# Graph and expert layer on one Trainium2 core: the slots of the routing's deviations and of the early rows' search

## Chip, core and metric

The kernel runs on one core of one Trainium2 chip. The metric is the device time of one execution in microseconds (us), the median of several runs.

## The reference

x is 4096 x 128, adj is 4096 x 4096 with few nonzero entries, thinly spread but denser in the first rows; all in fp32.

```python
h = layernorm(x)
filt = tanh(adj * adj) * (adj > 0)
vals, idx = top_k(filt, 350)                      # only rows with more than 350 entries lose any
new_adj = zeros.at[rows, idx].set(vals where kept)
x = x + relu(new_adj @ (tanh(h @ W_proj + b_proj) @ W_gcn) + b_gcn)
h = layernorm(x)
scores = h @ Wg.T + bg                            # 8 experts, best 2, softmax over the two
x = x + sum over e of combine[e] * (relu(h @ W1[e].T + b1[e]) @ W2[e].T + b2[e])
```

## The kernel before

**First stage: the adjacency in 64 chunks.** Rows of the output are worked in 8 blocks of 512 (`NB`), and each block needs 8 chunks (`NK`) of 512 x 512 of the adjacency. Chunk n, 1 MB, is loaded by SP into one of four buffers (`abuf`) once ACT has squared and DVE has marked chunk n - 4. ACT squares it (L1088) and takes the tanh (L1092) into `tbuf`, also four buffers; PE multiplies it by the features `g_sb`, four accumulating fp32 products of 128 x 512 (L1349); DVE marks its positive entries (`mark_positive`, L855 for a block's first chunk, L858 for the others), for the count of entries of each row. Every engine's program is written out by hand as a loop over **slots**, `for n in range(FFN)`, where slot n has chunk n and what else is due in that slot. Engines meet at semaphores alone, and each works strictly in the order of its own program. ACT squares chunk n + 1 in its slot n.

**Early rows.** Rows with over 350 entries need the exact top 350. They lie in the first block. Four of them are fetched, and a search of 15 steps (`STEPS`) finds each one's threshold, two bits a step: on DVE `raise_threshold` (L719, L721) takes the result of the step before, and `count_candidates` (L708, L712, L715) counts for three candidates; PE adds the counts up over the row's partitions (`total_candidates`, L1279), in the middle of the chunk's products in the same slot. Steps run in slots `STEP0` = 18 to 32. In slot `TIE` = 33 DVE counts the ties; in TIE + 1 it masks the rows (`mask_rows`, L735 to L740); in TIE + 2 PE turns them at the slot's head (`turn_rows`, L1289); in TIE + 3 and TIE + 4 it multiplies them by `g_sb` ahead of the chunk (`row_features`, L1294, 32 matmuls a slot); ACT copies the result in TIE + 4 (`features_out`, L1126), PE turns it in TIE + 6, and DVE writes it over the four columns of the features in TIE + 7 (`write_features`, L751). The first block itself is routed fifth and waits for this.

**Routing a block.** Once a block's features are finished, it is routed beside the chunks of later blocks. `ORDER` has the blocks, `START` the slot in which each begins: 19, 27, 35, 43, 47, 51, 58, 65. Blocks are counted here from 0, so routed block 2 is the third. From its START on, by slots: +0 PE turns the features (`features_back`, L1240); +1 DVE adds them to x, takes the statistics (L771, L775) and works out the deviations in 15 small linked instructions (`norm_scale`, L381 to L394); +2 DVE normalises the rows (`normalise`, L786), ahead of that slot's marks, and cuts them into two fp16 halves behind them (`cut_rows`, L798, L800); +3 PE turns them at the slot's head, and ACT copies them (L1138, L1140); +4 PE takes the gate's scores at the head (`gate`, L1320), DVE the best expert (`choose`, L805 to L812); +5 DVE the second, ahead of the marks (`choose_second`), ACT the exponential (L1144); +6 PE counts the places (`places`, L1327 to L1334), DVE the probabilities and the rows' slots in memory (`probabilities`, `assign`, L823 to L836). Then POOL scatters the block's rows with eight indirect DMAs (L623) to where the experts' tiles are read.

**Second stage: the experts.** After six blocks `first_tiles` on DVE, in slot `FIRST` = 58, works out the first 17 tiles of 256 rows. SP loads them into the place of `abuf` (L433, L435), after the marks of chunk 60. 39 tiles follow on PE (L1436 to L1458), from 319.4 us on, with the last two blocks' routing beside them. The results are scattered, loaded and added.

In a slot DVE has this order: `ready_steps` (a step of the search, `normalise`, `choose_second`), then `mark_positive`, then the rest (`route_steps`, and `first_tiles` last). PE has `row_features` and `route_steps` ahead of the chunk.

Of the kernel before, what the change touches and what calls it, by code (L numbers as in the profile page):

```python
# [7 lines left out]
CK = 4  # L8
# [6 lines left out]
def gnn_moe_layer(nc, x, adj_tiles, adj_rows, w_proj, b_proj, w_gcn, b_gcn,  # L15
# [43 lines left out]
    ORDER = list(range(1, NB // 2 + 1)) + [0] + list(range(NB // 2 + 1, NB))  # L59
    START = [19, 27, 35, 43, 47, 51, 58, 65]  # L60

    AT_ADD, AT_NORM, AT_TURN, AT_COPY, AT_GATE = 1, 2, 3, 3, 4
    AT_CHOOSE, AT_SECOND, AT_EXP, AT_PLACE, AT_PROB, AT_ASSIGN = 4, 5, 5, 6, 6, 6
    OUT = 1
    FIX = NK + OUT + 2
    STEP0 = FIX + 7
    TIE = STEP0 + STEPS
    FFN = NCH + 1

    COUNT = 2  # L70
    END = START[-1] + AT_ASSIGN + 1
    FIRST = START[SIX - 1] + AT_ASSIGN + 1
    NOWHERE = 1 << 20

    xs = nc.dram_tensor("routed_rows", (E * RS + TS, ROW), fp32).ap()
# [3 lines left out]
    with ctx:  # L79
# [576 lines left out]
        def _(dve):  # L656
            chain = [s_dve, 0]

            def link(ins):

                chain[1] += 1
                ins.then_inc(chain[0], 1)
                dve.wait_ge(chain[0], chain[1])
# [102 lines left out]
            def add_features(i, b, rs):  # L766
                at = space(i)

                dve.wait_ge(rs.r1, i + 1)
                xb = xres[:, b * SUB:(b + 1) * SUB, :]  # L770
                dve.tensor_tensor(xb, xb, at.x2[:, :].rearrange("p (c d) -> p c d", c=SUB), ALU.add  # L771
                                  ).then_inc(rs.x2, 1)
                dve.wait_ge(rs.x2, i + 1)
                for cc in range(SUB):
                    last = dve.bn_stats(stats[:, b * SUB + cc, :], xres[:, b * SUB + cc, :])  # L775
                link(last)
                norm_scale(dve, link, b * SUB, SUB).then_inc(rs.ns, 1)

            def normalise(i, b, rs):
# [163 lines left out]

            def ready_steps(n):

                if STEP0 < n <= TIE:
                    raise_threshold(early, 0, n - STEP0 - 1)
                if STEP0 <= n < TIE:
                    count_candidates(early, 0, n - STEP0)
                if n == TIE:  # L950
                    count_ties(early, 0)
                for i, b in enumerate(ORDER):
                    if n == START[i] + AT_NORM:
                        normalise(i, b, routed)
                    if n == START[i] + AT_SECOND:
                        choose_second(i, b, routed)

            def route_steps(n):
                for i, b in enumerate(ORDER):
                    if n == START[i] + AT_ADD:  # L960
                        add_features(i, b, routed)
                    if n == START[i] + AT_NORM:
                        cut_rows(i, routed)
                    if n == START[i] + AT_CHOOSE:
                        choose(i, b, routed)
                    if n == START[i] + AT_PROB:
                        probabilities(i, routed)
                    if n == START[i] + AT_ASSIGN:
                        assign(i, routed)

            for n in range(FFN):
# [54 lines left out]
            with dve.If(redo > 0):  # L1026
                chain[:], before_if = [s_dve2, 0], chain[:]
                dve.wait_ge(s_yo, NT)
                for i in range(2):
                    dve.wait_ge(routed.scat[i], NB // 2 * Q * 16)  # L1030
                link(dve.tensor_copy(base[:, :], base_i[:, :]))
                dve.tensor_tensor(key[:, :], flags[:, :], rowidf[:, :], ALU.mult).then_inc(s_key, 1)
                dve.wait_ge(s_keyrow, 16)
                link(dve.tensor_scalar(keyflag, keyrow, 0.0, None, ALU.is_gt))
                link(dve.tensor_reduce(nflag[:, :], keyflag, AX.X, ALU.add))

                link(dve.tensor_scalar(nflag[:, :], nflag[:, :], 1.0 / R, 0.5 - 0.5 / R, ALU.mult, ALU.add))
                dve.tensor_scalar(nrounds[:, :], nflag[:, :], 1.0, None, ALU.max).then_inc(s_nr, 1)
                rounds = read_rounds(dve)
                with dve.Fori(0, rounds) as r:  # L1040
                    pick_rows(general, r, keyrow)
                    square_rows(general, r)
                    for b in range(STEPS):
                        count_candidates(general, r, b)
                        raise_threshold(general, r, b)
                    count_ties(general, r)
                    mask_rows(general, r)
                    rows_turned(general, r)
                    write_features(general, r)
                dve.memset(tmp[:, :], 0.0).then_inc(s_fixed, 1)  # L1050
                dve.wait_ge(s_fixed, 1)
                dve.wait_ge(s_xre, 16)
                for i, b in enumerate(ORDER):
                    add_features(i, b, rerouted)
                    normalise(i, b, rerouted)
                    cut_rows(i, rerouted)
                    choose(i, b, rerouted)
                    choose_second(i, b, rerouted)
                    probabilities(i, rerouted)
                    assign(i, rerouted)  # L1060
                    if i == SIX - 1:
                        first_tiles()
                last_tiles()
                for t in range(NT, 2 * NT):
                    cut_h(t, t % 2)
                chain[:] = before_if
# [9 lines left out]
        def _(act):  # L1076
# [74 lines left out]

            def route_steps(n):
                for i in range(NB):
                    if n == START[i] + AT_COPY:
                        copy_norm(i, routed)
                    if n == START[i] + AT_EXP:
                        exp_diff(i, routed)

            for n in range(FFN):
# [77 lines left out]
        def _(pe):  # L1237
# [100 lines left out]
            def chunk_features(n):  # L1338
                ib, k, buf = n // NK, n % NK, n % NBUF
                if k == 0 and ib >= 2:  # L1340
                    pe.wait_ge(s_ev, ib - 1)
                if ib == 0:
                    pe.wait_ge(s_g, k + 1)
                pe.wait_ge(s_t, n + 1)
                for cc in range(CK):
                    c = k * CK + cc
                    if STEP0 <= n < TIE and cc == CK // 2:
                        total_candidates(early, 0, n - STEP0)
                    last = pe.matmul(ps_feat[ib % 2][:, :], g_sb[:, c, :], tbuf[:, buf, cc, :],  # L1349
                                     start=(c == 0), stop=(c == C - 1))  # L1350
                last.then_inc(s_pe, 1)
# [19 lines left out]
            def route_steps(n):  # L1371
                for i, b in enumerate(ORDER):
                    if n == START[i]:
# [3 lines left out]
                        if b == 0:  # L1377
                            pe.wait_ge(fixed_early, 1)
                        features_back(i, b, routed)
                    if n == START[i] + AT_TURN:  # L1380
                        normal_transpose(i, routed)
                    if n == START[i] + AT_GATE:
                        gate(i, routed)
                    if n == START[i] + AT_PLACE:
                        places(i, routed)

            for n in range(FFN):
# [159 lines left out]
```

## Time and profile before

| | |
|---|---|
| median of 3 runs (lowest to highest) | 465.27 us (464.77 to 466.58) |
| the profiled execution | 466.88 us, its span 465.1 us |
| busy PE, DVE, ACT, POOL | 400.0, 358.2, 339.2, 212.1 us |
| PE's idle time between 106 and 320 us, for DVE | 17.1 us |
| mean granted clock of PE | 0.958 |

A profile is one execution. Busy times and starts are us from the start of the span. The granted clock is the share of TensorE's full speed, 2.4 GHz, that was allowed in a stretch; its two levels are 1.2 and 2.4 GHz. The idle time of an engine is put down to what came last before it went on.

### The profile page before, as it was taken

Reading aid. Unit: us, or ns where it says so; the run is one execution under the profiler, and the core shown is the slowest. Engines: PE = TensorE matmul, PEld = TensorE weight load, DVE = VectorE, ACT = ScalarE, POOL = GpSimd, SP = SyncE. Lnnn points to the kernel's source line nnn. Section 1 sums busy time; section 2 is a strip of 40 time slices with the busy share of each in tenths; the row PEclk is TensorE's granted clock in tenths of the full one; section 3 lists DMA queues with packets and bytes.
Section 4 is the critical chain, followed back from the end, with each engine's and each line's share of the span. In section 5 each row is a group of like instructions: output and inputs, shape, how many; then the busy total and the mean of one; then the engine's idle time right before and its main releaser. Section 6 shows DMA issues by size and latency. Waiting matters only on the chain.

```text
span 465.1 us, 8214 instructions
## 1 busy us (share of the span) xinstructions
PE 400.0 (86%) x2552; PEld 245.2 (53%) x2552; DVE 358.2 (77%) x851; ACT 339.2 (73%) x345; POOL 212.1 (46%) x282
## 2 busy tenths in 40 slices
PE   0899999999699789999999979979898989999500
PEld 0455544444244244455454434437798989989500
DVE  5999978978999999984999999997886434444235
ACT  2789998889779867959999969973556656666400
POOL 3049961000003700730670648842777777777700
PEclk9999999999799979999999999989999999999955
DMA  7839996775375936874776758835635555441069
GB/s 227 329 118 374 341 336 216 255 278 206 144 261 200 298 122 249 304 259 183 286 253 256 261 185 320 276 125 76 110 97 148 108 102 121 91 78 51 18 217 327
DMA packets 57075, 95.44 MB, mean 205 GB/s; under 512 B 36740, under 2 KB 44088, under 8 KB 48832
## 3 DMA queue, kind: packets, MB, share of 16 engines
q1 hardware_dynamic: 45840, 79.80, 52.2%
q0 software_dynamic: 6048, 12.72, 9.3%
q10 hardware_dynamic: 5136, 2.30, 1.7%
q8 instruction: 25, 0.41, 0.4%
q14 instruction: 26, 0.21, 0.2%
HBM read 77.90 MB, written 12.67 MB: 195 GB/s over the span
## 4 chain that ended last, share of the span: by engine, by line
DVE 46%; PE 30%; issue 12%; DMA 5%; ACT 3%; POOL 2%; ACTq 1%; SPq 1%; DVEq 0%; POOLq 0%
DVE marks L858 17%; PE bank L1349 6%; PE bank L1436 3%; PE bank L1456 3%; PE bank L1437 3%; PE bank L1438 3%; PE bank L1457 3%; PE bank L1458 3%; ACT tbuf L1088 2%; DMA tbuf<-expert_rows 2%; DVE rowbf L712 2%; DVE nrm L786 2%; DVE w2h L866 2%; PE bank L1294 2%; DVE marks L855 1%
## 5 line engine op out<-in xcount | busy, mean ns | idle before, releaser
L1349 PE MATMUL bank<-tbuf,g_sb 128*128 128x512 f32 x512 | 239.7, 615 | 1.4 <-ACT g_sb L1108 0.7
L1349 PEld LDWEIGHTS bank<-tbuf,g_sb 128*128 128x128 f32 x512 | 95.6, 196 | 107.3 <-issue 101.4
L623 POOL DMA_INDIRECT routed_rows<-aug,slots x64 | 85.6, 1338 | 105.6 <-DVE base L836 88.0
L858 DVE SCALAR_TENSOR_TENSOR marks<-abuf,marks 128x2048 bf16<-128x2048 int32 x56 | 129.4, 2311 | 1.0
L1088 ACT ACTIVATE tbuf<-abuf 128x2048 f32<-128x2048 f32 x64 | 121.4, 1898 | 5.4 <-PE bank L1349 2.6
L1092 ACT ACTIVATE tbuf<-tbuf 128x2048 f32<-128x2048 f32 x64 | 122.3, 1911 | 2.0
L637 POOL DMA_INDIRECT expert_rows<-abuf,xmeta x78 | 76.9, 985 | 23.8 <-issue 22.0
L1009 DVE SCALAR_TENSOR_TENSOR tbuf<-bank,tbuf 128x512 f16<-128x512 f32 x78 | 50.2, 685 | 47.1 <-ACT tbuf L1195 47.0
L1456 PE MATMUL bank<-w2h,tbuf 128*128 x312 | 54.4, 220 | 2.0 <-DVE tbuf L1009 2.0
L1458 PE MATMUL bank<-w2h,tbuf 128*128 x312 | 54.3, 220 | 0.0
L1457 PE MATMUL bank<-w2l,tbuf 128*128 x312 | 54.3, 219 | 0.0
L1195 ACT ACTIVATE tbuf<-bank 128x512 f16<-128x512 f32 x78 | 46.3, 597 | 8.2 <-PE bank L1438 6.8
L1203 ACT ACTIVATE abuf<-bank,xmeta 128x128 f32<-128x128 f32 x78 | 24.4, 363 | 37.9 <-PE bank L1458 36.1
L1436 PE MATMUL bank<-abuf,w1h 128*128 128x256 f16 x156 | 42.6, 273 | 2.1 <-issue 2.0
L1437 PE MATMUL bank<-abuf,w1h 128*128 128x256 f16 x156 | 42.5, 273 | 0.0
L1438 PE MATMUL bank<-abuf,w1l 128*128 128x256 f16 x156 | 42.5, 273 | 0.0
L1456 PEld LDWEIGHTS bank<-w2h,tbuf 128*128 128x128 f16 x312 | 30.5, 98 | 2.9 <-issue 2.5
L1457 PEld LDWEIGHTS bank<-w2l,tbuf 128*128 128x128 f16 x312 | 30.5, 98 | 0.5
L1458 PEld LDWEIGHTS bank<-w2h,tbuf 128*128 128x128 f16 x312 | 30.5, 98 | 0.0
L526 POOL DMA_DIRECT2D wstage<-in_w x16 | 9.5, 595 | 41.6 <-DVE aug L670 24.4
L615 POOL COPY aug<-dest 128x4 int32<-128x4 int32 x16 | 8.6, 572 | 39.6 <-DVE aug L800 39.6
L1240 PE MATMUL bank<-ident,nrm 128*128 128x128 f32 x40 | 7.6, 322 | 15.6 <-DVE nrm L670 9.5
(212 smaller groups left out, 442.8 us busy)
## 6 DMA issues: line engine op xcount, KB each, us to landing
abuf<-in_adj_tiles SPq DMA_DIRECT2D x64, 1024.0 KB, 5.0
wstage<-in_w POOLq DMA_DIRECT2D x16, 256.0 KB, 6.0
tbuf<-expert_rows SPq DMA_DIRECT2D x8, 512.0 KB, 7.1
out<-xres ACTq DMA_DIRECT2D x8, 256.0 KB, 6.4
expert_rows<-abuf,xmeta POOLq DMA_INDIRECT x78, 2.5
routed_rows<-pad SPq DMA_DIRECT2D x9, 130.0 KB
routed_rows<-aug,slots POOLq DMA_INDIRECT x64
abuf<-routed_rows SPq DMA_TRANSPOSE x39
```

What stands on the lines that cost most here:

```text
L623: pool.indirect_dma_start(xs, bass.IndirectOffsetOnAxis(ap=slots[:, q, k * SUB + cc:k * SUB + cc + 1], axis=0), aug[:, q, k, cc, :], None) ...
L637: pool.indirect_dma_start(ys, bass.IndirectOffsetOnAxis(ap=xmeta[:, t % NT, s, 0:1].bitcast(i32), axis=0), ysb[:, u, s, :], None, bounds_c ...
L858: dve.scalar_tensor_tensor(mark, bits_in, 1.0, mark, ALU.min, ALU.add).then_inc(s_raw, 1)
L1088: act.activation(tbuf[:, n % NBUF, :, :], abuf[:, n % NBUF, :, :], ACT.Square).then_inc(s_sq, 1)
L1092: act.activation(tbuf[:, n % NBUF, :, :], tbuf[:, n % NBUF, :, :], ACT.Tanh).then_inc(s_t, 1)
L1349: last = pe.matmul(ps_feat[ib % 2][:, :], g_sb[:, c, :], tbuf[:, buf, cc, :], start=(c == 0), stop=(c == C - 1))
L1436: pe.matmul(dst, hi, xhl[:, u, 0, :], start=True, stop=False)
L1437: pe.matmul(dst, hi, xhl[:, u, 1, :], start=False, stop=False)
L1438: last = pe.matmul(dst, lo, xhl[:, u, 0, :], start=False, stop=True)
L1456: pe.matmul(dst, hs, hi, start=False, stop=False, skip_group_check=True)
L1457: pe.matmul(dst, hs, lo, start=False, stop=False, skip_group_check=True)
L1458: last = pe.matmul(dst, ls, hi, start=False, stop=(hb == HB - 1), skip_group_check=True)
```

## The change

The six blocks that are routed during the first stage (`SIX`) get one slot more between their addition and their normalisation: `norm_scale` is taken out of `add_features` into `scale_rows`, and runs in slot START + 2; `normalise` and all that follows move back by one slot, on all engines. The last two blocks keep their slots, with `scale_rows` in the slot of the addition, directly behind it. `FIRST` becomes 59, with `first_tiles` behind `scale_rows` of the seventh block in that slot; `END` stays.

The search makes no step in slots 21, 22, 29 and 30, START + 2 and START + 3 of the first two routed blocks. Its 15 steps are in slots 18 to 20, 23 to 28 and 31 to 36. `TIE` becomes 37, and all that follows the search comes four slots later; `write_features` is in slot 44 instead of 40. The third routed block has its deviations in slot 37 and its normalised rows in slot 38, those of TIE and of `mask_rows`.

```diff
-    AT_ADD, AT_NORM, AT_TURN, AT_COPY, AT_GATE = 1, 2, 3, 3, 4
-    AT_CHOOSE, AT_SECOND, AT_EXP, AT_PLACE, AT_PROB, AT_ASSIGN = 4, 5, 5, 6, 6, 6
+    def at(slot, spread=1):
+        return [slot + spread] * SIX + [slot] * (NB - SIX)
+
+    AT_ADD, AT_SCALE, AT_NORM, AT_TURN, AT_COPY, AT_GATE = at(1, 0), at(1), at(2), at(3), at(3), at(4)
+    AT_CHOOSE, AT_SECOND, AT_EXP, AT_PLACE, AT_PROB, AT_ASSIGN = at(4), at(5), at(5), at(6), at(6), at(6)
...
-    TIE = STEP0 + STEPS
+    SEARCH = [n for n in range(STEP0, NCH) if n not in (START[0] + 2, START[0] + 3, START[1] + 2, START[1] + 3)][:STEPS]
+    TIE = SEARCH[-1] + 1
...
-    END = START[-1] + AT_ASSIGN + 1
-    FIRST = START[SIX - 1] + AT_ASSIGN + 1
+    END = START[-1] + AT_ASSIGN[-1] + 1
+    FIRST = START[SIX - 1] + AT_ASSIGN[SIX - 1] + 1
...
                 link(last)
+
+            def scale_rows(i, b, rs):
                 norm_scale(dve, link, b * SUB, SUB).then_inc(rs.ns, 1)
...
-                if STEP0 < n <= TIE:
-                    raise_threshold(early, 0, n - STEP0 - 1)
-                if STEP0 <= n < TIE:
-                    count_candidates(early, 0, n - STEP0)
+                if n in SEARCH[1:]:
+                    raise_threshold(early, 0, SEARCH.index(n) - 1)
+                if n == TIE:
+                    raise_threshold(early, 0, STEPS - 1)
+                if n in SEARCH:
+                    count_candidates(early, 0, SEARCH.index(n))
...
                 for i, b in enumerate(ORDER):
-                    if n == START[i] + AT_ADD:
+                    if n == START[i] + AT_ADD[i]:
                         add_features(i, b, routed)
-                    if n == START[i] + AT_NORM:
+                    if n == START[i] + AT_SCALE[i]:
+                        scale_rows(i, b, routed)
+                    if n == START[i] + AT_NORM[i]:
                         cut_rows(i, routed)
...
                     c = k * CK + cc
-                    if STEP0 <= n < TIE and cc == CK // 2:
-                        total_candidates(early, 0, n - STEP0)
+                    if n in SEARCH and cc == CK // 2:
+                        total_candidates(early, 0, SEARCH.index(n))
...
-                    if n == START[i] + AT_GATE:
+                    if n == START[i] + AT_GATE[i]:
                         gate(i, routed)
-                    if n == START[i] + AT_PLACE:
+                    if n == START[i] + AT_PLACE[i]:
                         places(i, routed)
```

## Rows read from the trace of the kernel before

**Rows 1.** The page, part 4: the chain that ended last, by engine, by line.

```profile
DVE 46%; PE 30%; issue 12%; DMA 5%; ACT 3%; POOL 2%; ACTq 1%; SPq 1%; DVEq 0%; POOLq 0%
DVE marks L858 17%; PE bank L1349 6%; PE bank L1436 3%; PE bank L1456 3%; PE bank L1437 3%; PE bank L1438 3%; PE bank L1457 3%; PE bank L1458 3%; ACT tbuf L1088 2%; DMA tbuf<-expert_rows 2%; DVE rowbf L712 2%; DVE nrm L786 2%; DVE w2h L866 2%; PE bank L1294 2%; DVE marks L855 1%
```

**Rows 2.** Table of stretches: stretch and length, busy us (instructions) by engine, clock, DMA.

```profile
106.00:190.00 84.00, 72.84 (x250) 32.82 (x248) 79.15 (x203) 68.67 (x45) 15.27 (x14) 0.92 0.61 213
190.00:230.00 40.00, 39.90 (x186) 21.34 (x187) 31.24 (x67) 34.33 (x25) 15.94 (x12) 1.00 0.68 245
230.00:305.00 75.00, 68.89 (x269) 33.17 (x268) 70.06 (x207) 70.17 (x47) 44.36 (x36) 1.00 0.75 268
```

**Rows 3.** Waits of DVE, 106 to 318 us: what waited, for whom; total, times, longest.

```profile
DVE scores L805 <- PE bank L1320: 5.2, 1, 5.2
...
DVE feat_t L751 <- issue: 1.7, 1, 1.7
```

**Rows 4.** Waits of PE in the same stretch, the two longest groups.

```profile
PE bank L1279 <- DVE ncand L715: 10.2, 4, 4.7
PE bank L1240 <- DVE nrm L786: 6.0, 2, 3.1
```

**Rows 5.** Timeline of DVE, slots 20 to 24: start, us, line, operation, tiles, shapes.

```profile
117.40 0.68 DVE L771 TENSOR_TENSOR xres<-xres,bank 128x512 f32<-128x512 f32 x1
...
119.03 0.17 DVE L381 TENSOR_TENSOR mean<-stats 128x4 f32<-128x4 f32 x1
...
121.97 0.15 DVE L719 SCALAR_TENSOR_TENSOR okc<-bank,cand 128x4 f32<-128x4 f32 x1
...
123.61 1.11 DVE L786 TENSOR_SCALAR nrm<-xres,mean,rstd 128x128 f32<-128x128 f32 x4
124.63 2.29 DVE L858 SCALAR_TENSOR_TENSOR marks<-abuf,marks 128x2048 bf16<-128x2048 int32 x1
126.83 0.42 DVE L798 CAST aug<-nrm 128x508 f16<-128x508 f32 x1
...
127.89 0.15 DVE L719 SCALAR_TENSOR_TENSOR okc<-bank,cand 128x4 f32<-128x4 f32 x1
...
139.84 1.22 DVE L855 TENSOR_SCALAR marks<-abuf 128x2048 bf16<-128x2048 int32 x1
```

**Rows 6.** Timeline of DVE, slots 38 and 39, and slot 44.

```profile
203.64 4.68 DVE L858 SCALAR_TENSOR_TENSOR marks<-abuf,marks 128x2048 bf16<-128x2048 int32 x2
...
230.77 0.68 DVE L771 TENSOR_TENSOR xres<-xres,bank 128x512 f32<-128x512 f32 x1
```

**Rows 7.** Timeline of PE, slots 35, 37 and 43 to 45.

```profile
190.10 0.33 PE L1289 MATMUL bank<-ident,rowgt 128*128 128x128 f32 x1 [0.91 <-DVE rowgt L740]
...
201.45 3.66 PE L1294 MATMUL bank<-g_sb,row_t 128*4 128x128 f32 x32
...
228.52 10.47 PE L1349 MATMUL bank<-tbuf,g_sb 128*128 128x512 f32 x24
```

**Rows 8.** Timeline of PE, totals of slots 21, 29 and 30; in brackets the wait.

```profile
123.75 0.19 PE L1279 MATMUL bank<-ncand,same_row 128*128 128x4 bf16 x1 [4.20 <-DVE ncand L715]
...
164.12 0.19 PE L1279 MATMUL bank<-ncand,same_row 128*128 128x4 bf16 x1 [4.72 <-DVE ncand L715]
...
171.02 0.17 PE L1279 MATMUL bank<-ncand,same_row 128*128 128x4 bf16 x1
```

**Rows 9.** Table of stretches, behind three waits of PE: 4.7, 2.9 and 3.1 us.

```profile
164.00:171.00 7.00, 6.88 (x13) 3.25 (x14) 6.83 (x14) 2.77 (x4) 0.32 (x2) 0.57 0.34 131
274.00:281.00 7.00, 6.80 (x25) 3.87 (x26) 6.74 (x12) 3.42 (x4) 2.37 (x2) 1.00 0.48 162
305.60:312.00 6.40, 6.36 (x20) 3.35 (x20) 6.26 (x5) 4.47 (x5) 2.31 (x2) 0.73 0.13 31
```

**Rows 10.** Timelines of SP's queue and of PE: first tile load, first tile matmul.

```profile
309.32 1.33 SPq L433 DMA_TRANSPOSE abuf<-routed_rows  x1
...
319.44 0.27 PE L1436 MATMUL bank<-abuf,w1h 128*128 128x256 f16 x1
```

## What the change will do, predicted

> **What bounds the kernel now.** On the page PE is the busiest engine, but the chain that ended last runs 46% on DVE, 17% on one line, the marks of L858 [rows 1]. A share over the whole span can't say which engine limits a stage, so the table by stretches comes next [rows 2]. From 320 us on the tiles of the experts fill PE, and the change touches nothing there. In the three stretches from 106 to 305 us, slots 18 to 60, DVE shows 79.2 of 84, 31.2 of 40 and 70.1 of 75 us. Many of its instructions are short and linked by semaphores, and a few hundredths of a microsecond lie between them, which no busy time shows; so I read its timeline by starts, and the list of its waits [rows 3]: from its first search step at 106.4 us to slot 60 it stops twice, 5.2 us for the gate of the third routed block, and 1.7 us before L751, where it loads four registers. Everything else is its own work, end to end. PE waits for DVE: 10.2 us in four waits in the middle of search slots, 6.0 us in two for normalised rows [rows 4]. **The stage is bound by DVE's order of work**: its length is DVE's work plus DVE's own waits, and a wait of PE costs time only where it makes DVE wait later.
>
> **Prices on DVE**, start to start [rows 5]: addition and its statistics ADD 117.40 to 119.03 = 1.63; the scale SCALE 119.03 to 121.97 = 2.94; a search step RC (raise, then count) 121.97 to 123.61 = 1.64; NORM 1.02; marks M 124.63 to 126.83 = 2.20; CUT 126.83 to 127.89 = 1.06; the marks of a block's first chunk M0 1.22, less the 0.08 by which M too overlaps its follower = 1.13. Of two M in a row the second is 2.39 apart (4.68 for both [rows 6]).
>
> **The change part by part.** It adds and removes no instruction: the sum of DVE's work stays. Costed at nothing is the code for the redo, which did not run.
>
> (a) *SCALE apart from ADD, and one slot more for the first six blocks.* On DVE an M comes between ADD and SCALE. PE's transpose, gate and places, ACT's copy and exponential, and DVE's choices all move one slot back, so each handover keeps its distance. NORM now stands directly behind SCALE and waits for its semaphore, 0.1 us at most, by the same gaps.
>
> (b) *No search step in slots 21, 22, 29 and 30.* PE's waits in the middle of slots 21 and 29, 4.2 and 4.7 us [rows 8], go. What is late next: in slots 23 and 31 PE needs NORM, then that slot's candidates. DVE by starts from ADD at 117.40: M21 119.0, SCALE 121.2, NORM 124.2, M22 125.2, CUT 127.4, RC 128.4 to 130.1. PE is at the middle of chunk 23 near 127.6 and waits 2.5. DVE never stops in all this, so nothing is gained in time so far; PE's release is absorbed.
>
> (c) *The search ends four slots later: TIE is slot 37, not 33.* This decides. mask_rows stands in slot 38, and ahead of it on DVE, beyond what was there before, are four marks and the third block's ADD, SCALE and NORM: 4 x 2.20 + 1.63 + 2.94 + 1.02 = 14.4 us. PE's turn_rows, which waits for it, was at 190.10 [rows 7] and comes at 204.5. How long PE waits: counted back from there (MASK 1.4, M38, NORM, SCALE, M37, R and the ties 1.5, ADD, M36) the last candidates are ready at 189.4, and PE then does half a chunk and two more at 3.5 (24 matmuls took 10.47 [rows 7]): 198.1. So it waits about 6 us at the head of slot 39, where it waited 0.9. **That new wait takes the place of the two removed.** Behind it is the clock. In the stretch behind the 4.7 us wait the granted clock was 0.57, so mostly the lower level, 1.2 GHz; behind a wait of 2.9 us it was 1.00, behind one of 3.1 it was 0.73 [rows 4, 9]. The chunk and four transposes from 164.12 to 171.02 [rows 8] took 6.9 us; at full clock they are 3.5 + 0.44 and the small total: 2.8 lost. I take 2.8 for slot 39, as the row nearest in length of wait; the bounds are 1.7 (6.4 us at 0.73) and 5 (twice as much, if it should grow with the wait).
>
> From 204.5 PE has turn_rows 0.2, transposes 0.44, chunk 39 3.5 and 2.8 lost, row_features 3.6 (32 matmuls [rows 7]), gate 0.8: 215.8. This gate is what choose(2) on DVE needs. DVE is there at 204.5 + CUT 1.06 + M39 2.20 + rows_turned 0.2 + M0 1.13 = 209.1, so it waits 6.7 us, where it waited 5.2 [rows 3]. Then PE: chunk 40 3.5, counts 0.4, row_features 3.6, chunk 41 3.6, places 0.4 = 227.3. DVE meanwhile: CHOOSE 1.6, SECOND 1.1, M41 2.20, M42 2.39 = 223.1; the exponential on ACT stands behind features_out, which waits for the second row_features on PE (223.3), so 0.6 us; and assign(2) waits for places until 227.4, 3.0 us. **These two DVE waits the trace of before does not have.** From 227.4: the rest of assign 0.8, M43 2.20, M44 2.39, write_features 1.7 + 1.1 = 235.6 for ADD of the fourth block, which was at 230.77 [rows 6]. **The stage is then 4.8 us late.**
>
> (d) *Slots 44 to 60.* DVE had no wait there, and has the same instructions after, with as many pairs of marks. One handover tightens: gate(3) ends on PE, which is still catching up (from 227.3 five chunks and the transposes), at about 250.7, and DVE is there at 250.4: 0.3. first_tiles moves from ahead of the seventh block's ADD to behind its SCALE: same sum. SP's first tile load was at 309.3, PE's first tile matmul at 319.4 [rows 10]. The load needs marks 60 (5 us later) and the fifth block's scatters, which end on POOL near 313, so it comes at 315 to 317 and PE's tile near 323: still in time, at nothing; if the scatters take 4 us more, 1 to 2 us. NORM of the seventh block is 5.1 us late: 310.5 instead of 305.4.
>
> (e) *The end of the stage.* PE waited 3.1 us for that NORM and lost 1.7 to the clock behind it. Afterwards, by the same count, it waits about 3.0. (It also waits 6 us for NORM in slot 55; the clock lost there hides in the slack up to that block's gate.) If the clock holds, the tiles start 5.1 - 1.7 = 3.4 us late; if it falls, 5.1. Between 2.9 and 3.1 I can't tell and take the middle, **+4.3 us**. The tile stage follows unchanged.
>
> *A rule of the Trainium skill speaks against this.* Perfetto Trace Analysis, Optimization Strategies: when the matmul engine idles for others, work on those that block it, to keep it going. Read by it, the waits in slots 21 and 29 come off, 8.9 us, and the time is 456.4. The rows say that the blocker here has no gap itself.
>
> **Sum.** The profiled execution took 466.9 us, span 465.1, 1.6 above the median of 465.27. It would be 471.2, the median 465.3 + 4.3 = **469.6**.
>
> **The rivals.**
> *Faster: PE and ACT decide, and DVE has room that its starts don't show.* The two waits, 8.9 us, and twice 2.8 of clock come off; new are 2.5 in slots 23 and 31 each and a part of slot 39's: about -5, 460. For it: PE was busy 72.8 of the 84 us and ACT 68.7 [rows 2], so both wait for DVE a good deal. Against it: DVE's list of waits has nothing before the gate at 208.3. Chance 0.12.
> *No change: the wait at slot 39 costs less.* If PE keeps its clock behind it, gate(2) and places(2) come 2.8 sooner, ADD of the fourth block is 2.0 late and the tiles start 0.3 to 2 late: 465.6 to 467.3. Against it: each wait of over 3 us in this stage was followed by a lower clock. Chance 0.2.
> *Slower still: the clock falls in slots 23 and 31 too*, since 2.5 us follow there on another short wait. Then DVE's raise in slots 25 and 33 waits some 0.8 us each for PE's total, or the first tile loads are 1 to 2 late: 471 to 473. Chance 0.13.
> *The forecast*, 468 to 471: 0.55. That the change doesn't do what it says can't be: slots are constants, and each engine's order follows from them.
>
> **Range and chances.** 464.5 to 472.5 takes in all cases but the first, with some 0.12 below and 0.05 above. A measurement of this kernel can tell about 0.5%, 2.3 us, from no change: above 467.6 lie the forecast and the slower rival, 0.68; within 0.20; below 0.12.
>
> **What would show it.** Right: no DVE wait up to choose(2); turn_rows (L1289) at 204 to 205 behind a PE wait of about 6 us, with a low clock behind it; DVE waits of 6 to 7 us at L805 and 3 at L830; ADD of the fourth block near 235.6; tiles from 323. Wrong: L1289 before 202, a DVE wait in slots 23 to 36, or ADD of the fourth block before 231, which would mean a gain.

## The result, and the profile after

| | before | after |
|---|---|---|
| median, lowest to highest (4 runs each, same chip) | 465.55 us, 464.77 to 466.58 | 472.68 us, 470.88 to 473.63 |
| profiled execution, its span | 466.88 us, 465.1 us | 470.88 us, 469.1 us |
| mean granted clock, profiled | 0.958 | 0.961 |
| mask turned by PE (`turn_rows`) | 190.10 [rows 7] | 204.80 |
| gate of the third routed block on PE | 212.56 | 215.25 |
| addition of the fourth on DVE | 230.77 [rows 6] | 235.94 |
| first tile matmul | 319.44 [rows 10] | 323.39 |

The ratio after to before is 1.0142, 95% interval 1.011 to 1.0173: **slower**, by some 6.6 us. 469.6 was forecast. The median lies 0.2 us above the range (before's own median is 0.3 us higher here than the 465.27 that the forecast stood on), the profiled execution 0.3 below the 471.2 that was given for it. Two of the four runs of after took 470.88 and 471.75 at a mean clock of 0.961, two took 473.60 and 473.63 at 0.946 and 0.947.

The rows of after have other line numbers: marks L866 (a block's first chunk L863), `turn_rows` L1302, `row_features` L1307, gate L1333, places L1340 to L1347, candidates' total L1292, a chunk's products L1362, first tile L1449. First the waits of DVE and of PE from 100 to 325 us (total, times, longest), which answer to [rows 3, 4]:

```profile
DVE scores L813 <- PE bank L1333: 7.2, 2, 7.0
DVE place L838 <- PE bank L1347: 3.5, 2, 3.0
...
DVE feat_t L757 <- issue: 1.5, 1, 1.5
...
DVE p L831 <- ACT ex L1157: 0.5, 1, 0.5
```
```profile
PE bank L1292 <- DVE ncand L721: 8.0, 6, 2.5
PE bank L1253 <- DVE nrm L794: 7.4, 4, 3.3
PE bank L1302 <- DVE rowgt L746: 6.1, 1, 6.1
```

The two long waits of PE in the middle of slots 21 and 29 (4.20 and 4.72 [rows 8]) are gone, as the change has it. What came instead is six shorter ones of 8.0 us in all, where before had four of 10.2, one of 6.1 us for the mask, and more waiting for NORM: the groups of after add up to 22.2 us with a last one of 0.7, where PE waited 17.1 us for DVE before. Stretch table of after, cut at 190, 232 and 306 us so that it holds the whole lateness (columns as in [rows 2]), and the same two later stretches of before:

```profile
106.00:190.00 84.00, 73.89 (x265) 32.95 (x264) 79.50 (x192) 76.30 (x49) 17.23 (x15) 1.00 0.65 226
190.00:232.00 42.00, 35.88 (x169) 19.29 (x168) 29.83 (x72) 26.74 (x20) 12.45 (x9) 0.92 0.60 209
232.00:306.00 74.00, 71.01 (x272) 34.48 (x270) 67.49 (x200) 67.81 (x46) 41.47 (x33) 0.98 0.73 265
```
```profile
190.00:232.00 42.00, 41.90 (x191) 22.15 (x192) 33.20 (x71) 36.29 (x26) 17.63 (x13) 1.00 0.70 253
232.00:306.00 74.00, 67.25 (x268) 32.72 (x267) 69.09 (x205) 69.20 (x46) 43.23 (x35) 1.00 0.74 262
```

In the first stretch the clock is now 1.00 where it was 0.92, and PE was busy 73.89 us in place of 72.84: taking the long waits away did keep the clock. In the second PE was busy 41.90 of 42 us before; after, 35.88, and with the wait of 6.12 that makes the 42 again. So in both kernels PE has no gap there but the wait for the mask. That is where the time went. Timeline of PE in after, slots 39 to 48 (start, us, operation; in brackets the wait):

```profile
204.80 0.47 PE L1302 MATMUL bank<-ident,rowgt 128*128 128x128 f32 x1 [6.12 <-DVE rowgt L746]
205.06 1.06 PE L1253 MATMUL bank<-ident,nrm 128*128 128x128 f32 x4
205.92 5.81 PE L1362 MATMUL bank<-tbuf,g_sb 128*128 128x512 f32 x8
211.66 3.66 PE L1307 MATMUL bank<-g_sb,row_t 128*4 128x128 f32 x32
215.25 1.06 PE L1333 MATMUL bank<-gate_w,xnt 128*128 128x8 f32 x8
...
231.75 13.90 PE L1362 MATMUL bank<-tbuf,g_sb 128*128 128x512 f32 x32
...
249.79 0.95 PE L1333 MATMUL bank<-gate_w,xnt 128*128 128x8 f32 x8
```

The eight matmuls behind the wait took 5.81 us, where eight take 3.60 at full clock (a row of the kernel with slot 39 filled, below). Further on, at the end of the stage, the same pattern again, with NORM of the seventh block (compare the 3.1 us in [rows 4] and 0.73 in [rows 9]):

```profile
309.92 1.11 PE L1253 MATMUL bank<-ident,nrm 128*128 128x128 f32 x4 [3.33 <-DVE nrm L794]
310.82 4.56 PE L1362 MATMUL bank<-tbuf,g_sb 128*128 128x512 f32 x8
...
323.39 0.27 PE L1449 MATMUL bank<-abuf,w1h 128*128 128x256 f16 x1
```

### The profile page after: what moved, and what is told of

Same layout as the page of the kernel before. It is cut to its first block, busy times and chain, and to the rows that moved or that the text cites. A ratio compares the mean times of both kernels' runs of the same rounds, so it can differ in the third digit from the quotient of the medians.

```text
span 469.1 us, 8218 instructions
## 1 busy us (share of the span) xinstructions
PE 399.3 (85%) x2552; PEld 244.8 (52%) x2552; DVE 357.4 (76%) x851; ACT 339.5 (72%) x345; POOL 212.8 (45%) x282
## 4 chain that ended last, share of the span: by engine, by line
DVE 44%; PE 35%; issue 10%; DMA 5%; ACT 3%; POOL 2%; ACTq 1%; SPq 1%; POOLq 0%; DVEq 0%
DVE marks L866 17%; PE bank L1362 10%; PE bank L1449 3%; PE bank L1469 3%; PE bank L1451 3%; PE bank L1450 3%; PE bank L1470 3%; PE bank L1471 3%; ACT tbuf L1101 2%; DMA tbuf<-expert_rows 2%; DVE rowbf L718 2%; PE bank L1307 2%; DVE w2h L874 2%; DVE nrm L794 1%; DVE stats L683 1%
## 5 line engine op out<-in xcount | busy, mean ns | idle before, releaser
L1362 PE MATMUL bank<-tbuf,g_sb 128*128 128x512 f32 x512 | 238.6, 612 | 0.8 <-ACT g_sb L1121 0.7
L1362 PEld LDWEIGHTS bank<-tbuf,g_sb 128*128 128x128 f32 x512 | 95.2, 196 | 104.6 <-issue 98.7
L866 DVE SCALAR_TENSOR_TENSOR marks<-abuf,marks 128x2048 bf16<-128x2048 int32 x56 | 129.4, 2310 | 0.9
L643 POOL DMA_INDIRECT expert_rows<-abuf,xmeta x78 | 76.7, 984 | 24.0 <-issue 22.2
L1449 PE MATMUL bank<-abuf,w1h 128*128 128x256 f16 x156 | 42.6, 273 | 1.8 <-issue 1.8
L621 POOL COPY aug<-dest 128x4 int32<-128x4 int32 x16 | 9.6, 631 | 41.5 <-DVE aug L808 41.5
L1253 PE MATMUL bank<-ident,nrm 128*128 128x128 f32 x40 | 7.7, 325 | 17.1 <-DVE nrm L676 9.6
```

What stands on the lines that cost most here:

```text
L643: pool.indirect_dma_start(ys, bass.IndirectOffsetOnAxis(ap=xmeta[:, t % NT, s, 0:1].bitcast(i32), axis=0), ysb[:, u, s, :], None, bounds_c ...
L866: dve.scalar_tensor_tensor(mark, bits_in, 1.0, mark, ALU.min, ALU.add).then_inc(s_raw, 1)
L1449: pe.matmul(dst, hi, xhl[:, u, 0, :], start=True, stop=False)
```

## The experiments

My theory was the prediction's: the search ends four slots later, so the mask is late, PE waits for it and loses clock, and DVE, which bounds the stage, waits for PE. The rivals: the clock does most of it; or PE, not DVE, sets the end from the mask on. Times of a start are from the profile of that run. Each ratio is to the kernel before, run on the same chip beside it; its median was 465.95 in the first series, 466.1 in the second. In the third, every kernel's tile stage ran some 60 us longer, that of the kernel before too (526.3 us), while the first stage ran as ever; so of that series only ratios and starts in the first stage are used.

**Split alone**: the search has its old slots, the deviations have theirs alone.

```diff
-    SEARCH = [n for n in range(STEP0, NCH) if n not in (START[0] + 2, START[0] + 3, START[1] + 2, START[1] + 3)][:STEPS]
+    SEARCH = list(range(STEP0, STEP0 + STEPS))
```

> The slots of the deviations as in the changed kernel, the search in slots 18 to 32 as before (ties in slot 33). Theory (the late mask_rows costs, through PE's wait in slot 39 and two waits of DVE): turn_rows on PE is at 190 again, DVE waits about 7 us for gate(2) in slot 40, ADD of the fourth block is near 230.6, and the time is within 1 us of before, 464.5 to 466.5. Rival A (the split itself costs, one slot more of delay for each block): 468 or more with turn_rows at 190.

Measured 467.95 us, ratio 1.0055 (1.0033 to 1.0076), which misses the expectation. In its profile the tiles start at 319.34, as before, and the mask comes at 188.97. DVE's wait for the gate of the third block is gone; one of 5.5 us stands before `write_features` in its place (the profile calls it issue; register loads are part of it), and the gate of the fourth block has one:

```profile
DVE feat_t L757 <- issue: 5.5, 1, 5.5
...
DVE scores L813 <- PE bank L1333: 2.6, 1, 2.6
```

Of its ten runs, the three at a clock of 0.949 to 0.950 took 468.65 to 470.1, the seven at 0.961 or more 465.64 to 468.09. The clock explains a part; the rest of the 2 us isn't in the profile that I have, so what the split costs by itself stays open.

**Skip alone**: no step in the four slots, but the deviations stay in the slot of the addition.

```diff
-    def at(slot, spread=1):
+    def at(slot, spread=0):
```

> The search skips slots 21, 22, 29 and 30 as in the changed kernel, the deviations stay in the slot of the addition. Theory: turn_rows at 204 to 205 as with the whole change; gate(2) comes at once behind it, so DVE waits not there but some 9 to 10 us for places(2); ADD of the fourth block near 234, 3.4 us late; time 468 to 470. Rival A: within 1 us of before, as the split is not in it.

468.52 us, ratio 1.0057 (1.0037 to 1.0078), the time as expected. The mask comes at 205.57, the fourth ADD at 233.45, the first tile at 321.77. DVE's wait has moved to the places, where PE has both the gate and the two `row_features` ahead of them: 7.4 us, for 9 to 10 expected. So the late mask makes the stage late with or without the split. Each half costs about 0.55%; together they cost 1.4%.

**Half as much skipping**: only slots 21 and 22 have no step; the mask comes two slots sooner than in after.

```diff
-    SEARCH = [n for n in range(STEP0, NCH) if n not in (START[0] + 2, START[0] + 3, START[1] + 2, START[1] + 3)][:STEPS]
+    SEARCH = [n for n in range(STEP0, NCH) if n not in (START[0] + 2, START[0] + 3)][:STEPS]
```

> The whole change, but the search skips slots 21 and 22 alone (ties in slot 35). Theory: mask_rows is 4.4 us later than before, not 14.4: turn_rows near 194.5, PE waits some 3 us there; gate(2) near 215.4, DVE waits about 6 us for it and almost nothing for places(2); ADD of the fourth block near 231.3; time within 1.5 us of before, 465 to 467. Rival A: as the whole change, 470 or more.

465.40 us, ratio 1.0006 (0.9977 to 1.0036). Its profiled run is 2.05 us late from before the search on, so its starts are given less 2.05: mask 194.7 as expected, but the gate 213.5 and the fourth ADD 229.6, each some 2 us sooner than expected, and the first tile 319.0. The time is as expected: with half of the slots skipped no loss can be measured.

**The mask ahead of that slot's marks**: in slot 38 `mask_rows` goes ahead of `normalise` and the marks on DVE.

```diff
+                if n == TIE + 1:
+                    mask_rows(early, 0)
                 for i, b in enumerate(ORDER):
...
-                if n == TIE + 1:
-                    mask_rows(early, 0)
```

> The whole change, with mask_rows in slot 38 put ahead of that slot's normalised rows and marks on DVE, 3.2 us earlier in DVE's order, same work. Theory: turn_rows near 201.6 behind a PE wait of about 3 us; gate(2) and places(2) 3 to 5 us earlier; ADD of the fourth block near 232.5, 3 to 3.5 us earlier than 235.9; time 3 to 4 us below the whole change. Rival B (the wait of PE in slot 39 does not reach the end): no difference to the whole change.

468.99 us, ratio 1.0082 (1.0063 to 1.0101), 3.7 us below after. DVE had the mask ready 3.2 us sooner in its order, yet `turn_rows` came only 1.6 sooner, at 203.19 (wait 2.76), and the fourth ADD 1.8 sooner (234.15), where 3 to 3.5 were expected. Most of the rest went at slot 23. Timeline of PE in this kernel:

```profile
130.66 0.18 PE L1292 MATMUL bank<-ncand,same_row 128*128 128x4 bf16 x1 [2.53 <-DVE ncand L721]
130.69 2.45 PE L1362 MATMUL bank<-tbuf,g_sb 128*128 128x512 f32 x4
...
134.51 3.76 PE L1362 MATMUL bank<-tbuf,g_sb 128*128 128x512 f32 x4
...
138.06 0.21 PE L1292 MATMUL bank<-ncand,same_row 128*128 128x4 bf16 x1
```

The four matmuls from 134.51 took 3.76 us; in after, at the same place behind a wait of the same 2.53 us, they took 1.96. DVE then waited 1.4 us for that total. This is the event of the rival "slower still", in a kernel whose code up to there is after's. It came again in slot 31 (four matmuls 3.48 us at 169.28), where DVE did not wait. The first tile still came 3.2 us sooner (320.19): 1.4 us of that were won at the end of the stage, where the clock held behind a wait of 3.95 us. So the time came out as expected, by another sum.

**The clock at the mask**: 100 small products of constants, whose result nobody reads, fill PE's wait at the head of slot 39.

```diff
+            def keep_busy(count, blocks):
+                pe.wait_ge(routed.x2, blocks)
+                for _ in range(count):
+                    pe.matmul(bank[4][:, 0:P], ones_bf[:, :], before[:, :], start=True, stop=True)
...
+                if n == 39:
+                    keep_busy(100, 3)
```

> The whole change, with 100 small products of PE that nothing reads at the head of slot 39, ahead of its wait for the masked rows; they fill most of the 6.1 us. Theory: turn_rows stays at 204.8, but the clock does not fall behind it; the 2.8 us between it and gate(2) go, ADD of the fourth block is near 233.1 instead of 235.9, and the time falls by 2 to 3 us against the whole change. Rival C (the clock does not matter, DVE's order sets it all): no difference.

469.01 us, ratio 1.0068 (1.0038 to 1.0099). Timeline of PE and table of the stretch:

```profile
205.05 0.33 PE L1302 MATMUL bank<-ident,rowgt 128*128 128x128 f32 x1 [0.53 <-DVE rowgt L746]
205.21 0.60 PE L1253 MATMUL bank<-ident,nrm 128*128 128x128 f32 x4
205.65 3.60 PE L1362 MATMUL bank<-tbuf,g_sb 128*128 128x512 f32 x8
209.18 3.66 PE L1307 MATMUL bank<-g_sb,row_t 128*4 128x128 f32 x32
212.77 1.06 PE L1333 MATMUL bank<-gate_w,xnt 128*128 128x8 f32 x8
```
```profile
205.00:212.00 7.00, 6.95 (x39) 4.21 (x40) 4.55 (x5) 6.12 (x5) 2.31 (x2) 1.00 0.75 263
```

The mask comes when it came, but the clock stays at 1.00 (0.61 in after), and the gate and the fourth ADD come 2.5 us sooner (212.77 for 215.25, 233.45 for 235.94). That is the clock's price in slot 39; counted from the mask to the fourth ADD it is 31.1 less 28.4, 2.7 us.

**The clock everywhere**: the same also in the middle of slots 23 and 31 and at the heads of slots 55 and 61.

```diff
+                if n == 55:
+                    keep_busy(34, 6)
+                if n == 61:
+                    keep_busy(54, 7)
...
+                    if n in (23, 31) and cc == CK // 2:
+                        keep_busy(40, 1 if n == 23 else 2)
```

> As before, with such products also in the waits of slots 23 and 31 (40 each), 55 (34) and 61 (54). Theory: no fall of the clock anywhere in the first stage, so the tiles start 1 to 1.7 us earlier still, and the executions of this kernel lie closer together than those of the whole change (470.9 to 473.6 with mean clocks of 0.961 and 0.946), all at a mean clock of 0.97 or more: 467 to 469. Rival C: as warm_39, with the same spread.

467.12 us, ratio 1.0016 (0.9999 to 1.0034), and all ten runs have a mean clock of 0.972 to 0.976. They lie no closer together in time (465.9 to 468.6), against the expectation, so the clock is not all of the spread. Between the ratios 1.0142 and 1.0016 lie 1.3%, 5.9 us: with no fall of the clock, most of the loss is gone. That is no fair share of the change, though, since the kernel before has falls of its own that these products would also fill. **Before with two of them filled** (`keep_busy` as above):

```diff
+                if n == 54:
+                    keep_busy(46, 6)
+                if n == 61:
+                    keep_busy(54, 7)
```

> The kernel before, with small products of PE that nothing reads at the heads of slots 54 (46) and 61 (54), where it waits 2.9 and 3.1 us for normalised rows. Theory: the clock does not fall behind the wait in slot 61, 1.7 us less to the first tile: 463.5 to 464.5. If the clock there does not matter: no difference.

Ratio 1.0001 (0.9978 to 1.0023), which misses the expectation. The first tile is 0.7 us sooner (318.71), and the time doesn't show it. What the clock costs at the end of the stage in the kernel before is under what can be measured. What its falls in slots 21 and 29 cost was not tried.

**Who sets the stage from the mask on?** In this version of after `row_features` goes behind the routing's products, in slots 43 and 44, so that gate and places are not behind it. ACT's copies and PE's turn of the result move with it, to slots 44 and 45 (not shown).

```diff
-                if n == TIE + 3:
+                if n == 43:
                     row_features(early, 0, range(C // 2))
-                if n == TIE + 4:
+                if n == 44:
                     row_features(early, 0, range(C // 2, C))
...
-                if n == TIE + 7:
+                if n == 46:
                     write_features(early, 0)
```

> The whole change, with the 64 products row_features of PE moved from the heads of slots 40 and 41 to behind the routing's products in slots 43 and 44 (writing the features in slot 46). Theory: turn_rows at 204.8 behind the same wait of 6 us; gate(2) near 212.5, DVE waits 3 us for it instead of 7.0, and nothing for places(2) instead of 3.0; the tiles start 5 to 7 us earlier, at 317 to 318.5; time 464 to 466.5. Rival D (the late mask is all, where PE does the row_features is not): 470 to 472.

470.98 us, ratio 1.0096 (1.0074 to 1.0118), beside the faster two runs of after (470.88, 471.75): my theory fails here. The gate comes 3.5 us sooner, DVE's wait for it is halved, the fourth ADD comes 9.9 us sooner (226.07), and none of that reaches the tiles: 323.74, for 323.39. DVE's waits, then PE's timeline:

```profile
DVE scores L813 <- PE bank L1333: 6.3, 2, 3.4
DVE feat_t L757 <- issue: 6.2, 1, 6.2
```
```profile
211.78 0.95 PE L1333 MATMUL bank<-gate_w,xnt 128*128 128x8 f32 x8
...
224.49 3.66 PE L1307 MATMUL bank<-g_sb,row_t 128*4 128x128 f32 x32
...
231.71 3.66 PE L1307 MATMUL bank<-g_sb,row_t 128*4 128x128 f32 x32
...
250.12 0.95 PE L1333 MATMUL bank<-gate_w,xnt 128*128 128x8 f32 x8
```

PE runs without a gap from 204.86 to its gate of the fourth block at 250.12 (249.79 in after), whatever the order of the pieces. DVE waits 3.4, 6.2 and 2.9 us in turn, in place of 7.0 and 3.0. (The 6.2 us, called issue, stand before `write_features`. It needs the features that PE turned at 238.83 and ACT copied by 239.56, and then its register loads.)

**The same in the kernel before** (`row_features` in slots 41 and 42, the copies and the turn in 42 and 44, `write_features` in 45):

```diff
-                if n == TIE + 3:
+                if n == 41:
                     row_features(early, 0, range(C // 2))
-                if n == TIE + 4:
+                if n == 42:
                     row_features(early, 0, range(C // 2, C))
```

> The kernel before, with row_features moved from the heads of slots 36 and 37 to behind the routing's products in slots 41 and 42 (writing the features in slot 45). Theory: DVE's wait of 5.2 us for gate(2) goes, and with it the last wait of DVE but its register loads; the tiles start near 314.3 instead of 319.4; time 459.5 to 461.5. Rival D: 465 to 466.

465.18 us, ratio 0.9971 (0.9947 to 0.9996), far from the 5 us that I expected. The gate's wait is gone, and in its place the fourth ADD waits for PE's transposes, 2.0 us sooner than before:

```profile
228.75 0.69 DVE L771 TENSOR_TENSOR xres<-xres,bank 128x512 f32<-128x512 f32 x1 [5.68 <-PE bank L1240]
```

PE has no gap from 190.34 to 228. The first tile is not sooner (319.98): behind the wait for the seventh block's NORM eight matmuls took 6.06 us, for 5.30 in before.

**Half of PE's work for the early rows**: 32 of the 64 products of `row_features`, all in slot 41, so that the features of the four early rows are incomplete.

```diff
-                if n == TIE + 3:
-                    row_features(early, 0, range(C // 2))
                 if n == TIE + 4:
-                    row_features(early, 0, range(C // 2, C))
+                    row_features(early, 0, [0] + list(range(C // 2 + 1, C)))
```

> The whole change without 32 of the 64 products row_features (those at the head of slot 40), so the features of the four early rows lack half of their terms. Theory E (from turn_rows at 204.8 to gate(3) at 250.6 PE is itself without a gap, and its work in that stretch sets the end, wherever DVE spends its waits): 3.6 us less work of PE, so the tiles start 2.5 to 3.6 us earlier, at 320 to 321, and the time is 3 us below the whole change, 467 to 469. Rival F (DVE's order alone, as after_late seemed to say): no change against the whole change.

Ratio 1.003 (1.0011 to 1.005). Its mask was 1.7 us late (206.47; its clock had fallen behind slot 23). From the mask to the fourth ADD it took 26.3 us, after 31.1, and to the gate of the fourth block 40.2, after 45.0: 4.8 sooner for 3.6 us of products less and some 1.1 us less lost behind the mask (from the mask to the instruction behind the first chunk 5.7 us, after 6.9). The first tile is at 321.59, 1.8 us sooner for 2.5 to 3.6 expected, the late mask included. The order on DVE is untouched, so PE's work sets this stretch.

**The late mask by itself**: the kernel before, with its 15 steps in a row but four slots later (and one more wait of PE, on a semaphore that has long been reached).

```diff
-    STEP0 = FIX + 7
+    STEP0 = FIX + 11
```

> The kernel before, with the search in slots 22 to 36 without a gap and no split: ties in slot 37, as in the whole change (PE also waits at slot 19 for the split of the weights, long done). DVE saves the wait of 3.5 us for the early rows' values at 106.4, since the first step now comes later, so turn_rows should be at 201 to 201.5, 11 us later than before. Theory E: PE's work from turn_rows on then ends 3.5 us earlier than in the version that only skips, 465 to 467. Rival G (only a late turn_rows beyond PE's own pace matters, not the gap in the search): the same; if skipping itself costs, late_start is below 465.

Ratio 1.0024 (1.0 to 1.0047), 1.3 us. Mask at 203.88, 2 to 3 us later than expected, places waited for 7.4 us, fourth ADD 231.75, first tile 319.92. A mask 14 us late costs the kernel before only 1.0 us at the ADD and 0.5 at the tiles, where the change costs 5.2 and 4.0. Timeline of PE in slots 38 and 39:

```profile
195.51 0.18 PE L1283 MATMUL bank<-pair,same_row 128*128 128x1 bf16 x1 [2.28 <-DVE roweq L726]
...
197.12 1.12 PE L1240 MATMUL bank<-ident,nrm 128*128 128x128 f32 x4 [1.41 <-DVE nrm L786]
198.03 4.67 PE L1349 MATMUL bank<-tbuf,g_sb 128*128 128x512 f32 x8
203.88 0.33 PE L1289 MATMUL bank<-ident,rowgt 128*128 128x128 f32 x1 [1.18 <-DVE rowgt L740]
```

PE waits here too, but in three pieces, 4.9 us in all, and the clock is lower in the chunk ahead of the mask, not behind it. What the lateness costs can be read from the starts of the kernels on record:

| | mask | from it to the fourth ADD | to the fourth block's gate on PE | first tile |
|---|---|---|---|---|
| before | 190.10 | 40.67 | 52.59 | 319.44 |
| four slots later alone | 203.88 | 27.87 | 37.88 | 319.92 |
| skip alone | 205.57 | 27.88 | 37.87 | 321.77 |
| after, slot 39 filled | 205.05 | 28.40 | 42.27 | 321.00 |
| after | 204.80 | 31.14 | 44.99 | 323.39 |

In the order before, a late mask is followed by the fourth ADD 27.9 us later, with the gaps in the search or without them; so skipping costs there only through the mask. Before had 40.7 us between the two: the mask had 12.8 us of room. Of the 5.2 us that the ADD is late in after, 1.9 are the mask's 14.7 us less this room, 2.7 the clock behind the mask, and 0.5 what else the split does there. The split also puts one more chunk of PE's, 3.5 us, ahead of the fourth block's gate.

**A better version**: the kernel before, with `row_features` late and the small products at slots 54 and 61.

```diff
+                if n == 54:
+                    keep_busy(40, 6)
+                if n == 61:
+                    keep_busy(54, 7)
```

> The kernel before with row_features in slots 41 and 42 and the small products of before_warm. Theory: its first tile was at 320.0 in the profile behind a loss of 2.5 us to the clock, although NORM of the seventh block came 0.6 us sooner; with the clock kept, 461.5 to 463.5, below both kernels and with less spread. Rival: as before_warm.

Ratio 0.9964 (0.9946 to 0.9983), with the first tile at 317.52: faster than both kernels, by 0.4% or 1.9 us against before, where 2.6 to 4.6 us were expected.

## Why the prediction was right, and where it was wrong

**Right: the direction, the wait at the mask, the clock behind it, and nearly each start.** The mask was put at 204.5 and came at 204.80; PE's wait about 6, 6.12; the gate's end 215.8, 216.2; DVE's wait for it 6.7, 7.0; for the places 3.0, 3.04; for the exponential 0.6, 0.50; the fourth ADD 235.6, 235.94; its gate's wait 0.3, 0.24; the first tile load 315 to 317, 315.68; the first tile 323, 323.39. Here are the rows of DVE that the sum of part (c) stood on:

```profile
216.34 0.19 DVE L813 TENSOR_TENSOR scores<-bank,gate_b 128x32 f32<-128x32 f32 x1 [7.00 <-PE bank L1333]
...
227.87 0.22 DVE L838 TENSOR_TENSOR place<-bank,base 128x64 f32<-128x64 f32 x1 [3.04 <-PE bank L1347]
...
235.94 0.65 DVE L777 TENSOR_TENSOR xres<-xres,bank 128x512 f32<-128x512 f32 x1
```

Part (b) held too: NORM at 124.16 (124.2), the total of slot 23 behind a wait of 2.53 (2.5), and no wait of DVE up to `choose` of the third block.

**The clock's term**: 2.8 us were put down for slot 39, by the row of the 4.7 us wait. With the clock held there, the fourth ADD came 2.5 sooner, 2.7 counted from the mask; so the row was a fair price, and the bound of 5 was too wide.

**Wrong: "the stage is bound by DVE's order of work", read for the whole of it.** From the mask to the fourth block's gate it is PE's work that has no gap, before and after. [Rows 2] had it: PE busy 39.90 of 40 us from 190 to 230 before, DVE 31.24. I took DVE's two waits there as part of its own length and summed along DVE; summed on PE, the stretch is one wait, the clock behind it and PE's work. The starts came out right since I had also carried PE's queue from 204.5 to 227.4 and again to the gate at 250.7 (249.79 measured, its end 250.6). Experiments built on the sentence missed (`row_features` late in either kernel); the one built on PE's queue (half the products) went the way that it was expected to, if 1 us short at the first tile.

**Half right: the search's end "decides".** Four slots later alone cost the kernel before 0.24% (0 to 0.47%), since the mask had 12.8 us of room. The lateness beyond that room is 1.9 of the 5.2 us; the sum of part (c) never asked for the room, and came out because it carried the clock and the split's order along with the mask. In all the change leaves PE 22.2 us of waits for DVE in place of 17.1, with one of 6.12 us at the mask where the clock falls.

**Too small: the spread of the clock.** "Slower still", the clock falling in slots 23 and 31 too, was given 0.13, and the median lies in its 471 to 473, not in the 468 to 471 of the forecast. Two of the four runs of after have a mean clock of 0.946 and 0.947 and are 2.7 us above the profiled one; 0.015 of 470 us is 7 us of full speed, or 14 us more at the lower level; 2.7 of the 7 reached the end. Where it fell in those two isn't in their records; the profile of the kernel with the mask ahead shows it behind the waits of slots 23 and 31, with DVE waiting 1.4 us after the first, and with the small products in those slots too no run was below 0.972. That the fall was in these slots in after's two slower runs is not shown. The median of 472.68 stands between the two kinds of run, and this is what took it past my range. A forecast made for the profiled execution needs such falls added for the median.

**Part (e)** was between: the wait was to be 3.0 and was 3.33, the clock behind it fell in part (0.77 from 309.9 to 316), PE began on the seventh block's NORM 4.3 us late (309.92 for 305.64) for 5.1, and the tiles started 3.95 late for 4.3. In **slot 55** PE was to wait 6 us and waited 2.30. I had set DVE's lateness there against a PE on time, but PE's own gate of the fourth block was 7.1 us later than before (249.79 for 242.69), one chunk of it by the change. That is argued. Behind the 2.30 us the clock fell (eight matmuls took 5.30 us), and DVE did not wait for that block's gate: it cost nothing in the sum, as the text said.

**A rule of the Trainium skill.** PE's two waits came off, 8.9 us, and the kernel is 1.4% slower: the measurement decides against the 456.4 us. Perfetto Trace Analysis, Optimization Strategies, in the Trainium skill speaks of the engines that are "blocking the critical path". The change made no engine faster and took no work off DVE; it moved the wait, so this run does not test that sentence as it stands. Perfetto Trace Analysis, Optimization Strategy, in the Trainium skill says that a kernel can have several regimes with another engine contended in each. The stretches of this stage bear that out: before, up to 190 us DVE is busy 79 of 84 us, from 190 to 232 PE 41.90 of 42.

## What to carry to other kernels

For each stretch find the engine whose busy time and one wait fill it, and sum along that one; the other engine's waits are then only where its slack shows. Here the waits that were taken off PE came back at later handovers, since DVE's work was moved and not shortened: look for the instruction that stands behind the moved work (here the mask), ask how much room it has before anyone waits for it (12.8 us), and price what lies beyond with the clock behind it. Where a program's executions differ in their granted clock, forecast the median from several runs, not from the profiled one.

## What the runs showed of the hardware

**The same wait does not always cost the clock.** Behind 2.53 us in slot 23, four matmuls took 1.96 us in after and 3.76 in the kernel with the mask ahead. Waits for NORM show the same. Full clock is 3.60 us for the eight matmuls behind it. 2.30 us lowered it in after, and 3.95 did not in the kernel with the mask ahead:

```profile
281.37 0.66 PE L1253 MATMUL bank<-ident,nrm 128*128 128x128 f32 x4 [2.30 <-DVE nrm L794]
281.86 5.30 PE L1362 MATMUL bank<-tbuf,g_sb 128*128 128x512 f32 x8
```
```profile
308.09 0.66 PE L1253 MATMUL bank<-ident,nrm 128*128 128x128 f32 x4 [3.95 <-DVE nrm L794]
308.58 3.60 PE L1362 MATMUL bank<-tbuf,g_sb 128*128 128x512 f32 x8
```

2.29 us in the kernel with the mask ahead left it alone too, and so did 2.91 in before, at 1.00 [rows 9]; 1.98 with the skip alone (5.29 us), 3.09 in the kernel before with `row_features` late (6.06) and 3.90 with the split alone (5.29) lowered it. Length alone doesn't tell. The four transposes straight behind the wait don't either: they took 0.66 us in both rows above. TensorE: Matmul & The Clock Gate, Part 1, in the Trainium skill says that how many matmuls run slow at a kernel's start differs between runs of the same kernel. The two pairs of after's runs (0.961, 0.946) also differ; no run here shows whether by the same cause.

**Small products hold it.** Some 34 to 100 bf16 products of 128 x 128 with constants, in a wait that is there anyway, kept the clock at full behind them in the profiles of these kernels. The 100 of slot 39 took 5.75 us, and the mask came 0.25 us later with them (205.05 for 204.80).
